# A depthwise convolution on TensorE: block-diagonal Toeplitz weights read with a step, and x by channel straight from memory

## The reference

```
y[b, t, c] = sum over k of cond[k, c] * x[b, t - 31 + k, c]      # causal depthwise conv, 32 taps, rows before t = 0 are 0
x  = x + y
ada = cond @ ada_w + ada_b                                       # shift1, scale1, gate1, shift2, scale2, gate2, one row for each batch
x1 = layernorm(x) * (1 + scale1) + shift1
q, k, v = x1 @ qkv_w + qkv_b                                     # 16 heads of 128
a  = softmax(q k^T / sqrt(128)) v   per batch and head           # 32 x 32 scores
z  = x + gate1 * (a @ out_w + out_b)
x2 = layernorm(z) * (1 + scale2) + shift2
out = x + z + gate2 * (gelu(x2 @ ffn_w1 + ffn_b1) @ ffn_w2 + ffn_b2)
```

## Time and profile before

| | |
|---|---|
| Median of three runs | 334.75 us (332.64 to 336.67) |
| Profiled execution | 332.91 us |
| Its span, first to last instruction | 331.1 us |
| TensorE busy | 305.3 us, 92% of the span |
| TensorE weight loads busy | 258.3 us, 78% |
| VectorE, ScalarE, GpSimd busy | 46%, 47%, 24% |
| First projection matmul (L986) starts | 48.32 us |
| Chain that ended last | 84% TensorE, 8% VectorE, 3% "issue", 2% DMA |

### The profile page before, as it was taken

How to read it: one execution, slowest core, us unless ns; L and a number is a source line. 1 busy time by engine, 2 the same in 40 slices (tenths; PEclk the granted TensorE clock), 3 DMA queues, 4 the chain that set the end, 5 groups by cost and what they waited for, 6 DMA issues and landing times.

```text
span 331.1 us, 7543 instructions
## 1 busy us (share of the span) xinstructions
PE 305.3 (92%) x3279; PEld 258.3 (78%) x3279; DVE 151.1 (46%) x237; ACT 155.2 (47%) x259; POOL 80.6 (24%) x70
## 2 busy tenths in 40 slices
PE   0854989999999999999999999999999999999994
PEld 0854879788888888888888888888888787688884
DVE  4612283366324326327224432432534799773232
ACT  3333323555266444536525526634543647742910
POOL 8200077120063020034103006302003345420400
PEclk9999998999999999999999999999999999999998
DMA  6780023010023002004202001400100000000011
GB/s 204 194 317 6 4 79 113 4 65 0 2 65 107 21 2 63 2 0 129 63 0 63 0 0 63 128 2 2 63 2 1 2 2 0 0 2 0 0 65 63
DMA packets 10056, 15.74 MB, mean 48 GB/s; under 512 B 837, under 2 KB 6061, under 8 KB 9901
## 3 DMA queue, kind: packets, MB, share of 16 engines
q1 hardware_dynamic: 9712, 15.24, 14.6%
q10 hardware_dynamic: 317, 0.10, 0.1%
HBM read 14.26 MB, written 1.11 MB: 46 GB/s over the span
## 4 chain that ended last, share of the span: by engine, by line
PE 84%; DVE 8%; issue 3%; DMA 2%; ACT 0%; ACTq 0%; POOL 0%
PE bank L986 17%; PE bank L987 17%; PE bank L988 17%; PE bank L1062 8%; PE bank L995 4%; PE bank L996 4%; PE bank L997 4%; PE bank L1048 3%; PE bank L893 2%; PE bank L922 2%; DMA crow<-in_cond_dram 2%; PE bank L958 2%; PE bank L908 1%; PE bank L877 1%; DVE yacc L786 1%
## 5 line engine op out<-in xcount | busy, mean ns | idle before, releaser
L308 POOL TENSOR_TENSOR wl<-raw,wh 128x512 fp32r<-128x512 f32 x40 | 52.3, 1331 | 163.5 <-ACT wh L367 163.5
L986 PE MATMUL bank<-x1h,wl 128*128 128x512 f32 (+1 forms) x176 | 67.4, 383 | 1.5 <-DVE x1l L640 1.5
L442 ACT ACTIVATE pool<-bank,bg 128x512 f32<-128x512 f32 x56 | 38.6, 689 | 58.3 <-PE bank L988 58.1
L987 PE MATMUL bank<-x1l,wh 128*128 128x512 f32 (+1 forms) x176 | 65.9, 374 | 0.0
L988 PE MATMUL bank<-x1h,wh 128*128 128x512 f32 (+1 forms) x176 | 65.8, 374 | 0.0
L698 DVE SCALAR_TENSOR_TENSOR ol<-bank,bT,oh 128x512 fp32r<-128x512 f32 x32 | 24.0, 749 | 49.9 <-ACT oh L471 48.9
L986 PEld LDWEIGHTS bank<-x1h,wl 128*128 128x128 f32 x176 | 33.8, 192 | 7.6 <-DVE x1l L640 1.6
L988 PEld LDWEIGHTS bank<-x1h,wh 128*128 128x128 f32 x176 | 33.9, 193 | 5.7
L987 PEld LDWEIGHTS bank<-x1l,wh 128*128 128x128 f32 x176 | 33.9, 193 | 5.6 <-issue 0.2
L1062 PEld LDWEIGHTS bank<-pt,pool 128*128 128x128 f32 x256 | 31.9, 191 | 3.4 <-DVE pt L687 0.8
L1062 PE MATMUL bank<-pt,pool 128*128 128x128 f32 x256 | 32.8, 276 | 0.6 <-DVE ol L698 0.4
(11 more groups left out here) (110 smaller groups left out, 429.3 us busy)
## 6 DMA issues: line engine op xcount, KB each, us to landing
raw<-in_L_cond_qkv_w_dram SPq DMA_DIRECT2D x12, 512.0 KB, 3.9
raw<-in_L_cond_out_w_dram SPq DMA_DIRECT2D x4, 512.0 KB, 3.6
raw<-in_L_cond_ffn_w_dram SPq DMA_DIRECT2D x4, 512.0 KB, 3.4
pool<-in_x_dram SPq DMA_DIRECT2D x2, 512.0 KB, 4.2
pool<-cond_padded SPq DMA_DIRECT2D x4, 256.0 KB, 4.7
adaw<-in_L_cond_ada_w_dram SPq DMA_DIRECT2D x1, 1024.0 KB, 7.7
out_dram<-pool SPq DMA_DIRECT2D x4, 256.0 KB, 2.2
adaw<-in_L_cond_ada_w_dram SPq DMA_DIRECT2D x1, 512.0 KB, 6.3
```

Source lines behind the costliest of these rows:

```text
L308: g.tensor_tensor(wl[:, cols], raw[:, cols], wh[:, cols].bitcast(F32), ALU.subtract)\
L442: a.activation(dst, src, ACT.Identity, bias=bg[:, j // GH, j % GH:j % GH + 1])\
L986: pe.matmul(dst, wl[:, w_cols], a_hi, start=start, stop=False)
L987: pe.matmul(dst, wh[:, w_cols], a_lo, start=False, stop=False)
```

## The change

x is loaded with input times on the partitions, straight into group g's 32 partitions, all four groups, from a view with 64-channel pieces (`x_v` is now `b t c -> t b c`); the spreading copies and the zeroed `x_by_channel` are gone. `toep` is now the zeroed tile: each group's rows land in their own 32 partitions and their own part of the row, so that with zeros elsewhere the weights of a slot, `toep[:, :, :, c]`, are a full 128x128 block-diagonal matrix. They are read with a step of 64 elements, and nothing is turned. `conv(k)` makes one product for each slot, 64 in all, and adds into a bank that already holds x: four products with `pick` as weights put it there, in the order of output times that the Toeplitz rows have. `turn(n)` no longer adds to transposed x and starts its own accumulation.

The order changes too. SP issues the padded `cond` ahead of x and the Toeplitz DMAs ahead of `adaw`; two of the x DMAs go to ACT. `modulation(0)` is cut into a part with scale1 (now 0) and one with shift1 (now 1), behind the convolution and behind `turn(1)`; `turn(3)` and the old `modulation(1)` move between the projections. The first four low weight parts stand ahead of `rstd(0)` on GpSimd, and two go to VectorE.

```diff
-        pick = sb("pick", [P, 2, CT, T])
+        pick = sb("pick", [P, CT, 2, T])
...
-        with nc.sbuf_tensor("x_by_channel", [P, QB, SLOTS, QB, B // QB], F32) as xq:
+        with nc.sbuf_tensor("toep", [P, QB, T, SLOTS], F32) as toep:
             pass
...
-        xtok = pool[:, 6144:8192].rearrange("p (n c) -> p n c", c=C)
-        toep = pool[:, 0:2048].rearrange("p (s u) -> p s u", u=T)
-        toep_in = pool[:, 2048:4096].rearrange("p (u s) -> p u s", u=T)
+        xq = pool[:, 0:2048].rearrange("p (b s) -> p b s", b=B)
...
-        ADA_PARTS = [(0, ADA1), (ADA1, 2 * ADA1), (2 * ADA1, ADA)]
-        ADA_BANKS = [YB[1], OB[1], YB[1]]
-        ADA_STEPS = [1, 3, 4]
+        ADA_PARTS = [(CT, 2 * CT), (0, CT), (ADA1, 2 * ADA1), (2 * ADA1, ADA)]
+        ADA_BANKS = [YB[0], YB[0], OB[1], YB[1]]
+        ADA_STEPS = [1, 3, 4, 5]
...
-        x_v = x.rearrange("(n q) t c -> (q t) n c", q=QB)
+        x_v = x.rearrange("b t c -> t b c")
...
-            for n in range(HALVES):
-                sp.dma_start(xtok[:, 4 * n:4 * n + 4, :], x_v[:, 4 * n:4 * n + 4, :]).then_inc(s_x[n], 16)
+            sp.dma_start(pad_rows(0, T), cond.rearrange("k (g s) -> k g s", g=QB)).then_inc(s_pad, 16)
+            for g in (0, 1):
+                sp.dma_start(xq[T * g:T * (g + 1), :, :], x_v[:, :, SLOTS * g:SLOTS * (g + 1)]).then_inc(s_x, 16)
+            sp.wait_ge(s_pad, 32)
+            for g in (0, 2, 1, 3):
+                sp.wait_ge(s_tz[g // 2], g % 2 + 1)
+                sp.dma_start(toep[T * g:T * (g + 1), g, :, :].rearrange("p u s -> p (u s)"),
+                             bass.AP(cond_pad, g * (2 * T - 1) * SLOTS, [[SLOTS, T], [1, T * SLOTS]]))\
+                    .then_inc(s_toep, 16)
             load_adaw(0, 0, ADA1 * P)
             for at, src in ((B_QKV, qkv_b), (B_ADA, ada_b), (B_OUT, out_b), (B_F1, ffn_b1), (B_F2, ffn_b2)):
                 n = src.shape[0] // P
                 sp.dma_start(rows[at:at + n, :], src.rearrange("(n p) -> n p", p=P)).then_inc(s_row[1], 16)
-            sp.wait_ge(s_pad, 32)
-            for g in range(QB):
-                sp.dma_start(toep_in[T * g:T * (g + 1), :, :].rearrange("p u s -> p (u s)"),
-                             bass.AP(cond_pad, g * (2 * T - 1) * SLOTS, [[SLOTS, T], [1, T * SLOTS]]))\
-                    .then_inc(s_toep, 16)
+            load_group(0)
             load_adaw(1, ADA1 * P, ADA * P)
-            load_group(0)
...
             for q in (2, 3):
-                g.memset(xq[:, q, :, :, :], 0.0).then_inc(s_xz[1], 1)
+                g.memset(toep[:, q, :, :], 0.0).then_inc(s_tz[1], 1)
...
-            for i, q in SPREADS_POOL:
-                g.tensor_copy(xq[T * q:T * (q + 1), q, :, i, :],
-                              xtok[T * i:T * (i + 1), :, SLOTS * q:SLOTS * (q + 1)].rearrange("p n s -> p s n"))\
-                    .then_inc(s_xq[2], 1)
...
+            low_parts(0, range(0, 4))
             rstd(0)
-            low_parts(0, range(0, 4))
+            g.wait_ge(s_vlow, 2)
+            g.wait_ge(s_wlo, 4)
+            g.sem_inc(s_wlo, 2)
             rstd(1)
-            low_parts(0, range(4, 6))
...
-            a.dma_start(pad_rows(0, T), cond.rearrange("k (g s) -> k g s", g=QB)).then_inc(s_pad, 16)
             a.wait_ge(s_zr, 1)
             a.dma_start(pad_rows(T, 2 * T - 1), zrows[:, :].rearrange("k (g s) -> k g s", g=QB)).then_inc(s_pad, 16)
+            for g in (2, 3):
+                a.dma_start(xq[T * g:T * (g + 1), :, :], x_v[:, :, SLOTS * g:SLOTS * (g + 1)]).then_inc(s_x, 16)
             a.dma_start(crow[:, :], cond).then_inc(s_row[0], 16)
...
-            a.wait_ge(s_toep, 16 * QB)
-            for k in (1, 3):
-                blk = slice(CBLK * k, CBLK * (k + 1))
-                a.activation(toep[:, blk, :].rearrange("p s u -> p u s"), toep_in[:, :, blk], ACT.Copy)\
-                    .then_inc(s_tp[k], 1)
-            conv_copy(0)
+            high_parts(0, range(0, 2))
             conv_copy(2)
-            high_parts(0, range(0, 4))
+            high_parts(0, range(2, 6))
+            group_biases(0, 0, 3)
             xc_copy(0)
-            group_biases(0, 0, 3)
             squares(0)
-            xc_copy(2)
-            high_parts(0, range(4, 6))
             squares(1)
             x1_high(0)
+            xc_copy(2)
...
+            conv_copy(1)
+            conv_copy(3)
             v.wait_ge(s_btc, 1)
             modulation(0)
             one_plus(0, SCALE1)
-            conv_copy(1)
-            conv_copy(3)
+            for p in (4, 5):
+                cols = slice(PIECE * p, PIECE * (p + 1))
+                v.wait_ge(s_whi, p + 1)
+                v.tensor_tensor(wl[:, cols], raw[:, cols], wh[:, cols].bitcast(F32), ALU.subtract).then_inc(s_vlow, 1)
+            centre(0)
             xc_copy(1)
-            centre(0)
+            modulation(1)
             scale_up(0)
             var_eps(0)
             centre(1)
             norm(0)
             shift(0)
             x1_low(0)
-            modulation(1)
...
-            for n in range(NX):
-                pe.wait_ge(s_x[n // 2], 16)
-                for i in range(2 * CT):
-                    ct, t = divmod(i, 2)
-                    pe.matmul(XB[n][:, P * i:P * (i + 1)], xtok[:, 2 * n + t, ct * P:(ct + 1) * P], ident[:, :],
-                              start=(i == 0), stop=False, is_transpose=True, skip_group_check=True)
...
+            pe.wait_ge(s_const, 4)
+            pe.wait_ge(s_x, 16 * QB)
+            for k in range(NX):
+                if k == NX - 1:
+                    pe.wait_ge(s_cond, 1)
+                pe.matmul(CB[k][:, :], pick[:, :, :, :].rearrange("p k a u -> p (k a u)"),
+                          xq[:, :, CBLK * k:CBLK * (k + 1)].rearrange("p b s -> p s b"),
+                          start=True, stop=False, skip_group_check=True)
...
                 for s in range(CBLK):
                     c = CBLK * k + s
-                    for j in range(QB):
-                        m = pe.matmul(CB[k][T * j:T * (j + 1), B * s:B * (s + 1)], toep[:, c, :],
-                                      xq[:, j, c, :, :].rearrange("p i n -> p (i n)"), start=True, stop=True)
+                    m = pe.matmul(CB[k][:, B * s:B * (s + 1)], toep[:, :, :, c].rearrange("p j u -> p (j u)"),
+                                  xq[:, :, c], start=False, stop=(s == CBLK - 1), skip_group_check=True)
                 m.then_inc(s_cv, 1)
...
-            for k in range(NX):
-                conv(k)
+            conv(0)
+            conv(1)
+            pe.wait_ge(s_row[1], 16 * 5)
+            pe.transpose(XB[0][:, 0:NBIAS], rows[:, :], ident[0:NBIAS, 0:NBIAS]).then_inc(s_bt, 1)
+            conv(2)
+            conv(3)
+            pe.wait_ge(s_adaw[0], 16)
+            modulation(0)
+            pe.wait_ge(s_btc, 1)
             turn(0)
+            mean(0)
             turn(1)
-            mean(0)
-            turn(2)
+            pe.wait_ge(s_adat, ADA_STEPS[0])
+            modulation(1)
             var(0)
             mean(1)
             spread(0)
-            pe.wait_ge(s_adaw[1], 16)
-            modulation(1)
-            turn(3)
+            turn(2)
             var(1)
...
             project_chunk(0, (0, 1))
             spread(1)
+            pe.wait_ge(s_xc[0], 2)
             project_chunk(0, (2,))
-            pe.wait_ge(s_co[1], 2)
+            turn(3)
+            pe.wait_ge(s_adaw[1], 16)
             modulation(2)
             project_chunk(0, (3,))
-            pe.wait_ge(s_adat, ADA_STEPS[1])
+            modulation(3)
+            pe.wait_ge(s_adat, ADA_STEPS[2])
             mean(2)
```

More of the change, by code:

```diff
@@ L136, in pad_rows @@
             return bass.AP(cond_pad, r0 * SLOTS, [[SLOTS, r1 - r0], [(2 * T - 1) * SLOTS, QB], [1, SLOTS]])
-        SPREADS = [(i, g) for g in range(QB) for i in range(QB)]
-        SPREADS_ACT, SPREADS_POOL = SPREADS[0::4], SPREADS[2::4]
-        SPREADS_DVE = SPREADS[1::2]
-        s_x = [sem(f"x_half{n}_loaded") for n in range(HALVES)]
+        s_x = sem("x_loaded")
         s_toep = sem("toeplitz_loaded")
-        s_tp = [sem(f"toeplitz_block{k}_turned") for k in range(NX)]
-        s_xz = (sem("x_by_channel_zeroed_by_vector"), sem("x_by_channel_zeroed_by_gpsimd"))
-        s_xq = (sem("x_by_channel_by_scalar"), sem("x_by_channel_by_vector"), sem("x_by_channel_by_gpsimd"))
+        s_tz = (sem("toeplitz_zeroed_by_vector"), sem("toeplitz_zeroed_by_gpsimd"))
+        s_xi = sem("x_in_conv_banks")
         s_zr, s_pad = sem("zero_rows_set"), sem("cond_padded_written")
@@ L408, in x1_high @@
                     a.activation(part(x1h, ct, NORMS[n]), ln_c(n, ct), ACT.Copy).then_inc(s_hi, 1)
-            for n in range(HALVES):
-                a.wait_ge(s_x[n], 16)
-            a.wait_ge(s_xz[0], 2)
-            a.wait_ge(s_xz[1], 2)
-            for i, g in SPREADS_ACT:
-                a.activation(xq[T * g:T * (g + 1), g, :, i, :],
```

(25 more changed lines are left out.)

45 lines of the change are left out of this document (10 added, 35 removed).

## The result

The changed kernel took 352.87 us (median of four runs, 349.79 to 353.24) against 333.69 for the kernel before on the same chip (the three runs of the table and a fourth): ratio 1.054, 95% interval 1.046 to 1.063. It is slower, as forecast, and inside the range, but the forecast step of 9 us was 17 in the profiled execution (349.79, span 347.9) and 19 between the medians. Some executions of one and the same kernel are over 1.5% slower than its fastest; the medians here count them, the ratios and intervals leave them out.

What follows compares the result with a forecast made beforehand. TensorE was taken as the bound, running without a gap from its first projection at 48.32 us. Delay to `turn(0)` 7.7, normalisation -1.6 and moved work +3.0 made +9.1 on 332.91: 342 us, range 328 to 354.

Steps and rivals of the forecast that it cites:

- (d): Convolution: 23.2 us, 40 records at 112 ns before the clock falls, 88 at 213 ns after; end at 39.3 us.
- (b): Loading of x: in 256 B pieces it lands at 9 to 11.5 us, taken as 10.
- (c): Four products of x: 6 us, from 10 to 16, raising the clock on the way.
- B: Rival: 256 B steps in weights and x cost TensorE, nothing to +23 us; half gives 354; chance 0.11.
- The clock: TensorE's clock rises behind dense products, not transposes or `modulation(0)`, and falls a few microseconds into the convolution; chance 0.58.
- (e): From the convolution to `turn(0)`: it starts at 41.1 us, 7.7 us late, with no supply stall left.
- (f): Normalisation: reordered work sums to -1.6 us, putting TensorE's first projection at 54.4 us.
- (g): Behind the first projection: `turn(3)` and a modulation of 16 records, moved between projections, add 3.0 us.
- Rival A: The clock stays up through the convolution, 15.7 to 30.0 us; total 327 to 329 us; chance 0.22.
- C: Rival: small pieces cost twice 19.6 ns, x lands 5 us later; 347 us; chance 0.09 together with D.
- D: Rival: stalls were not supply, new convolution up to 7 us longer; 349 us; chance 0.09 together with C.

Runs made afterwards that it cites:

- crow_first: The changed kernel with the small load of `cond` issued first on ACT's queue instead of behind x: 352.19 us, ratio 1.049 to the kernel before.
- fold_small: The changed kernel without its four x products (x added through the tap of lag 0), each slot made as four 32x32 products: 338.05 us, ratio 1.010.
- fold_1small: fold_small, but only block 0 of the convolution uses 32x32 products and the other three blocks two 64x64 products per slot: 331.07 us, ratio 0.988.
- small: The changed kernel with each slot's block-diagonal product made as four 32x32 products out of the same tile: 337.88 us, ratio 1.016.
- fold_2small: fold_small, but blocks 1 and 3 use two 64x64 products per slot, blocks 0 and 2 still 32x32 ones: 335.10 us, ratio 0.997.

## Why the prediction was wrong in size

The direction, the place and most steps held; the size was off by 7.7 us of span (16.8 measured, 9.1 forecast). The step that failed is (d), the convolution: it put the cost of the step in the weights at nothing and gave the records at 2.4 GHz 112 ns; they took 217. By the prediction's own steps:

- *(b) x at 10.* Wrong by 2.6 us: 12.57. Half of it was the small load of `cond`, which stands last on ACT's queue (crow_first: 11.29 without it). SP's wait ended at 6.58 and not at 8, so that Toeplitz rows were already under way then; that these are what held it up is likely, but no run separates it. The other half is x.
- *(c) the products of x, 6 us.* Wrong by 1.05: 7.05. The clock did rise on the way, at 17.8, and gave nothing, since the moving operand has the step too (0.43 us apart without it, in the run with both contiguous).
- *(d) the convolution, 23.2 us.* Wrong by 4.4: 27.6. I took B's lower end, "nothing, since fp32 weights come slowly", and so gave the 40 records before the clock's fall 112 ns. With the step they take 217 ns at either clock: the convolution is 27.6 us whether the clock is up for 1.6 us of it (here) or 3.6 (crow_first), and 23.2 with contiguous weights and 4.5 us. That end was right at 1.2 GHz (217 against 213) and wrong at 2.4. By sizes: contiguous weights with the clock up for 1.6 us would take 14 x 0.112 + 114 x 0.213 = 25.9 (an estimate), so 1.7 of the 4.4 us are the step as the clock went in this execution, and 2.7 its earlier fall. With the step in, though, the moment of the fall changes nothing, so the step alone accounts for all 4.4. Whether it makes the clock fall earlier is open, but it need not: counted from its rise the clock stood at 2.4 GHz for 3.4 us in the changed kernel, and for 6.8 in crow_first, which has the step too, and in both runs with contiguous weights. The upper end, a factor of 1.8 on all of it, was near the truth at 2.4 GHz (217 / 112 = 1.9) and wrong at 1.2, where almost all of the time was spent.
- *The clock.* Right: it rose behind the dense products and fell in the convolution, in this kernel and in the one with contiguous weights. With a dense product ahead of each slot it stayed up for the whole convolution. One reading in it was too strong: that transposes and `modulation(0)` do not raise it. In the run with GpSimd's order alone it rose behind the same transposes, in the middle of `modulation(0)`. The group of loads of 13.6 to 17.2 us there, against the 333 ns of the earlier trace rows:

```profile
L958 PEld LDWEIGHTS bank<-condT,adaw 128*128 128x128 f32 x16 | 2.5, 241 | 0.0
```

- *(e) `turn(0)` 1.8 us behind the convolution, without a supply stall.* Right: 47.26 to 49.08.
- *(f) the normalisation, 13.3 us.* 12.55. `mean(0)` 4.7 us after `turn(0)` (4.6 forecast); the clock rose in `turn(1)` at 55.4, so `modulation(1)` and `var(0)` took 2.0 instead of up to 3.4. `shift(0)` took 0.42 an instruction, near the 0.38 said; the run of the kernel before with this alone shows it to be GpSimd's order (at most 1.9 us of 2.8 reached the first projection).
- *(g) +3.0 behind the first projection.* +3.5. The moved work cost 2.9, and the stretch at 1.2 GHz near the first projections went away (1.6 us given back). Against that came 1.7 us that I had no term for, the stall in the scores product, and 0.5 that I can't place. The stall goes with where TensorE's list is cut into packets of 256 instructions: the runs whose list is half a packet longer (the four with dense products) or one and a half shorter than fold_small's (fold_1small) have none; the changed kernel and the six others of its family have 1.7 to 2.4 us, and the two lists of the kernel before none. But the list does not settle it alone: in the changed kernel the stall stands in the third group of heads, in crow_first and the two runs with contiguous weights, whose lists are as long, in the fourth. Why a packet is fetched late at one place and not at another is open.
- *Beyond the profile.* The medians differ by 2 us more than the profiled executions. Three other executions of the changed kernel show a lower mean clock (0.940 to 0.941 against 0.947), and crow_first, with 0.941 too, shows one way to it: the low clock lasts into the normalisation. It is not the whole cause, since a fifth execution had 0.949 and a span of 350.0, 2.1 us over the profiled one; that stays open.

Rival A did not happen, and would have needed a free step as well: at 2.4 GHz throughout, and with the dense products in it, the convolution took 30.2 us with the step and 23.5 without. Rival B was half the truth: the step costs, but at 2.4 GHz alone. That its 354 lies so near the 352.87 is luck, since it spread the price over all of the convolution and the products of x. C had the right sign, and x itself gave 1.3 of its 5 us; but its price did not occur. ACT's queue, which carries half of x, in crow_first from 0 to 12 us:

```profile
q10 hardware_dynamic: 2253, 0.59, 26.6%
```

That is 0.266 x 16 x 12 / 2253 = 22.7 ns a packet, not twice 19.6. D is excluded: the new convolution had no stall.

## What to carry to other kernels

Cost a matmul with few moving columns by its weight load first: with 32 of them, 128 contiguous columns of fp32 weights took 112 ns at 2.4 GHz and 213 at 1.2, two records to a matmul. Four diagonal blocks side by side (13.6 us here) are worth more than one full matrix that is mostly zeros (27.6), though the number of instructions runs into the supply; making three of the four blocks of slots out of 64x64 products avoided the stalls (13.1 against 15.3 with 32x32 alone). Other mixes were not run. When an operation is priced by its like, ask separately at each clock what the difference in address pattern costs.

## What the runs showed of the hardware

- A step of 8 B in fp32 weights cost TensorE 1% (0.371 us a slot against 0.367), one of 16 B the full price (0.491), 256 B nearly the same (0.471), at 2.4 GHz. At 1.2 GHz 256 B cost 2% (217 against 213 ns).
- Advanced Engine Details and Errata (SBUF Cachelines) of the Trainium skill speaks of lines of 16 bytes: at least two hits on a line absorb the latency, and the tolerance for a step hangs on the type. The runs at 2.4 GHz agree, for fp32 weights: two to a line at 0.371 us a slot, one at 0.491.
- 512 moving columns of fp32 with a step of 256 B took 0.86 us a record at 1.2 GHz and at 2.4, contiguous 0.43 at 2.4.
- TensorE got through 222 or 223 records before its first stall (the kernel before: 35 ahead of the convolution and 187 in it; small: 10 and 213; fold_small: 2 and 221; fold_2small: a short wait after 223), and from then on was stopped after every 128 or so: its instructions come in packets of 16 KB, 256 to a packet, and it went on 1.2 to 1.6 us after one had landed. A list of many short products is bound by them.
- A stall of that kind turned up about 100 us further on (at 138 to 167 us), in a loop that was not touched, in 7 of the 12 kernels with a changed list ahead of it and not in the other 5. Behind 3 of the 7 the clock fell to 1.2 GHz for another 3.4 us.
